# Sixteen layer norms, six gated feed-forwards and two half additions, rewritten block by block, in a single-core transformer kernel

## The chip, the cores and the metric

The kernel runs on one core of a Trainium2 chip. The metric is the device time of one execution, in microseconds. PE is the matrix engine (TensorE), DVE the vector engine, ACT the scalar engine, POOL the general engine (GpSimd) and SP the engine whose queue issues most DMAs. PE, DVE, ACT and POOL each run their own instructions in order and wait for each other through semaphores.

## The reference, cut to what matters

Four layers work on a stream `x` of 16 sequences of 256 tokens with 128 channels. Each layer is feed-forward, attention, feed-forward, each on a layer norm of the stream; the feed-forwards are added at one half.

```python
def _layernorm(x, axis=-1, eps=1e-05):
    m = jnp.mean(x, axis=axis, keepdims=True)
    v = jnp.var(x, axis=axis, keepdims=True)
    return (x - m) / jnp.sqrt(v + eps)
...
# layer 1's feed-forward: two layers, each window attention and then
h = shift_token(x)
mu = h.mean(-1, keepdims=True)
var = h.var(-1, keepdims=True)
h = (h - mu) / jnp.sqrt(var + 1e-05) * lg + lb
h = h @ w1 + b1
a, g = jnp.split(h, 2, axis=-1)
h = a * jax.nn.gelu(g, approximate=False)
x = x + h @ w2 + b2
...
# layer 3's feed-forward
gate = jnp.einsum('bsd,hd->bsh', x, wg)
up = jnp.einsum('bsd,hd->bsh', x, wu)
h = jax.nn.silu(gate) * up
return jnp.einsum('bsh,dh->bsd', h, wd)
...
x = x + 0.5 * _L1_ffn_ref(_layernorm(x, axis=-1), ...)
```

`shift_token` takes the upper 64 channels from the token before (zero for a sequence's first).

## The kernel before

The stream lies in SBUF as `X`, 128 channels on the partitions and 4096 tokens along them; its norm goes to `XN`, of the same shape. Work on tokens goes in `NBLK` = 8 blocks of `BLK` = 512, which is also one PSUM bank in f32. The kernel is a row of phases (class `Phase`): each takes its buffers and semaphores, writes out one program for each engine, and ends in a barrier of all engines. So nothing of a phase overlaps the next, and the time of the kernel is the sum of its phases and of the gaps between them. Every order inside a phase is written out by hand; no scheduler moves anything.

`layer_norm` is called 16 times: 12 plain norms (tags `l0a_norm`, `l0att_norm` and so on, for the six feed-forwards and attentions of layers 0 and 1 and the six of layers 2 and 3), and 4 learned norms inside layer 1's feed-forwards (tags `l1a_ln0`, `l1a_ln1`, `l1b_ln0`, `l1b_ln1`; the profile writes `l1a_ln` and `l1b_ln` for them, the number left out). A plain norm does, for each block s: a matmul with `ones_mean` puts the mean over channels on all partitions of `stat` (L252, PE), DVE subtracts it (`dev`, L269), ACT squares (`sq`, L283), a second matmul gives the variance (L255), ACT takes the logarithm (`log`, L288) and its exponential at -0.5 (`inv`, L291), DVE multiplies (`XN`, L277). PE runs all eight means and then all eight variances; DVE all eight `dev` and then the products; ACT all eight squares, then in each half four logarithms and four exponentials. A learned norm first copies its input to `hs` with the upper 64 partitions shifted by a token (L261 and L262, both on DVE), multiplies by `lg` as well (L274), and ACT adds `lb` in eight last instructions (L296).

`gated_ffn` is called 6 times, 4 times as "gelu" (`l1a_ff`, `l1b_ff`; hidden size 341, in three chunks of 128, 128 and 85) and twice as "int8" (`l3a`, `l3b`; hidden size 384). A loop of 4 trips does `U` = 2 blocks each: for each block and chunk two matmuls `G` and `UP` (L1482, L1483), the gate on ACT (L1500 or L1503), a product on DVE (`hid`, L1530 or L1533); for each block three matmuls back (`OUT`, L1472) and the addition to the stream on DVE (L1518 or L1520). The next trip starts after the second of these additions (`trip_done`). After both of layer 1's inner layers, `add_half` is a phase of its own in which DVE adds half of `XN` to `X` in one instruction of 4096 columns (L1545).

## Time and profile before

| | us |
|---|---|
| median of three runs (6445.07 to 6453.1) | 6449.81 |
| the profiled execution, its own time | 6449.29 |
| its span, first to last instruction | 6447.5 |
| PE busy (32011 matmul instructions) | 4952.8 |
| DVE busy | 4378.2 |
| ACT busy | 3259.1 |
| POOL busy | 2307.3 |

A duration is that of one instruction; where like instructions follow each other, the profile merges them to one row with a count, and the row's duration runs from the first's start to the last's end. An f32 matmul of 512 columns is two PE instructions in the records, so eight of them read x16. What stands in brackets is the idle time of the engine before a row and what ended it. The clock is that which was granted to PE, as a share of its full 2.4 GHz.

### The profile page before, as it was taken

Reading aid. Unit: us, or ns where it says so; the run is one execution under the profiler, and the core shown is the slowest. Engines: PE = TensorE matmul, PEld = TensorE weight load, DVE = VectorE, ACT = ScalarE, POOL = GpSimd, SP = SyncE. Lnnn points to the kernel's source line nnn. Section 1 sums busy time; section 2 is a strip of 40 time slices with the busy share of each in tenths; the row PEclk is TensorE's granted clock in tenths of the full one; section 3 lists DMA queues with packets and bytes.
Section 4 is the critical chain, followed back from the end, with each engine's and each line's share of the span. In section 5 each row is a group of like instructions: output and inputs, shape, how many; then the busy total and the mean of one; then the engine's idle time right before and its main releaser. Section 6 shows DMA issues by size and latency. Waiting matters only on the chain. (4 is left out here: it accounts for less than half of the span.)

```text
span 6447.5 us, 112356 instructions
## 1 busy us (share of the span) xinstructions
PE 4952.8 (77%) x32011; PEld 3318.9 (51%) x32108; DVE 4378.2 (68%) x10756; ACT 3259.1 (51%) x6903; POOL 2307.3 (36%) x1555
## 2 busy tenths in 40 slices
PE   6777888777769879869969879866678657596777
...
GB/s 29 0 0 3 298 287 283 191 0 0 0 11 0 3 11 0 0 9 1 1 11 0 4 11 0 4 8 7 37 17 1 3 12 13 40 0 14 0 0 17
DMA packets 162590, 213.89 MB, mean 33 GB/s; under 512 B 54804, under 2 KB 90984, under 8 KB 162408
## 3 DMA queue, kind: packets, MB, share of 16 engines
...
## 5 line engine op out<-in xcount | busy, mean ns | idle before, releaser
L1841 POOL TENSOR_TENSOR l0b_S<-l0b_sim 128x1024 f32<-128x1024 f32 x256 | 494.1, 1967 | 135.4 <-ACT l0b_sim L1904 113.7
L1841 POOL TENSOR_TENSOR l0a_S<-l0a_sim 128x1024 f32<-128x1024 f32 x256 | 494.2, 1967 | 83.4 <-ACT l0a_sim L1904 62.6
L1876 PE MATMUL l0b_WT<-ident,l0b_w 128*128 128x128 f32 x2048 | 268.9, 287 | 64.0 <-DVE l0b_w L1974 59.4
L1876 PE MATMUL l0a_WT<-ident,l0a_w 128*128 128x128 f32 x2048 | 269.1, 287 | 63.5 <-DVE l0a_w L1974 58.6
L1974 DVE SCALAR_TENSOR_TENSOR l0b_w<-l0b_S,l0b_best,l0b_SG 128x1024 f32<-128x1024 f32 x256 | 311.2, 1276 | 8.3 <-ACT l0b_SG L1921 4.4
L1974 DVE SCALAR_TENSOR_TENSOR l0a_w<-l0a_S,l0a_best,l0a_SG 128x1024 f32<-128x1024 f32 x256 | 311.2, 1276 | 8.2 <-ACT l0a_SG L1921 4.5
L1876 PEld LDWEIGHTS l0b_WT<-ident,l0b_w 128*128 128x128 f32 x2048 | 240.4, 148 | 107.3 <-DVE l0b_w L1974 107.3
L1876 PEld LDWEIGHTS l0a_WT<-ident,l0a_w 128*128 128x128 f32 x2048 | 240.4, 148 | 106.9 <-DVE l0a_w L1974 106.9
L1921 ACT ACTIVATE l0b_SG<-l0b_S 128x1024 f32<-128x1024 f32 x256 | 260.5, 1026 | 55.1 <-DVE l0b_w L1974 50.3
L1921 ACT ACTIVATE l0a_SG<-l0a_S 128x1024 f32<-128x1024 f32 x256 | 260.5, 1026 | 54.1 <-DVE l0a_w L1974 48.9
L2288 ACT ACT_TABLE_LOAD x16 | 20.5, 1283 | 511.6 <-issue 305.5
L772 ACT ACTIVATE l0att_XS<-l0att_XP 128x768 f32<-128x768 f32 x256 | 224.9, 879 | 71.3 <-PE l0att_XP L613 67.7
L793 ACT ACTIVATE l0att_E<-l0att_S,l0att_least 128x256 f32<-128x256 f32 x512 | 232.2, 503 | 29.8 <-DVE l0att_least L861 29.5
L869 DVE COPY l0att_ET<-l0att_TU 128x512 f32<-128x512 f32 x256 | 176.2, 688 | 89.9 <-PE l0att_TU L637 88.9
L861 DVE CUSTOM_DVE_ANT_0 l0att_S<-l0att_SC,l0att_BD 128x256 f32<-128x256 f32 x512 | 196.7, 419 | 29.7 <-issue 24.7
L1251 ACT ACTIVATE l1a_att_E<-l1a_att_S,l1a_att_nmax 128x192 f32<-128x192 f32 (+1 forms) x512 | 195.5, 418 | 10.3 <-DVE l1a_att_nmax L1350 10.3
L1251 ACT ACTIVATE l1b_att_E<-l1b_att_S,l1b_att_nmax 128x192 f32<-128x192 f32 (+1 forms) x512 | 195.4, 418 | 10.3 <-DVE l1b_att_nmax L1350 10.3
L793 ACT ACTIVATE l1att_E<-l1att_S,l1att_least 128x128 f32<-128x128 f32 (+1 forms) x512 | 192.0, 448 | 13.6 <-DVE l1att_least L861 13.6
L1058 POOL TENSOR_TENSOR l1a_att_E<-l1a_att_E,l1a_att_rec 128x768 f32<-128x768 f32 (+1 forms) x96 | 154.5, 1610 | 111.4 <-DVE l1a_att_rec L1359 111.4
L1058 POOL TENSOR_TENSOR l1b_att_E<-l1b_att_E,l1b_att_rec 128x768 f32<-128x768 f32 (+1 forms) x96 | 154.5, 1610 | 111.2 <-DVE l1b_att_rec L1359 111.2
L2375 PE MATMUL l2bc_OUT<-l2bc_hot,l2bc_part 128*128 128x512 bf16 x752 | 167.7, 383 | 16.3 <-DVE l2bc_hot L2407 13.1
L2375 PE MATMUL l2ac_OUT<-l2ac_hot,l2ac_part 128*128 128x512 bf16 x752 | 166.6, 381 | 16.0 <-DVE l2ac_hot L2407 13.1
...
## 6 DMA issues: line engine op xcount, KB each, us to landing
shifted_rows<-l0att_XS SPq DMA_DIRECT2D x256, 384.0 KB, 3.2
l0att_BD<-shifted_rows SPq DMA_DIRECT2D x256, 256.0 KB, 3.4
...
```

Source lines behind the costliest of these rows:

```text
L772: act.activation(XS[:, j % 2, t, :, :].rearrange("p c h -> p h c"), XP[:, :, 0:WIN], ACT.Copy).then_inc(sm["x_kept"], 1)
L793: act.activation(E[:, j % 2, h, t, 0:keys(t)], S[:, j % 2, h, t, 0:keys(t)], ACT.Exp, bias=least[:, j % 2, h, t:t + 1], scale=-1.0).then_i ...
L861: dve.tensor_tensor_reduce(S[:, j % 2, h, t, 0:keys(t)], SC[:, h, t, 0:keys(t)], add, -scale, 3e38, ALU.add, ALU.min, least[:, j % 2, h, t ...
L869: dve.tensor_copy(ET[:, j // 2 % 2, 2 * (j % 2) + h, :, :], TU[:, h % NT, 0:len(blocks), :]).then_inc(sm["et_copied"], 1)
L1058: pool.tensor_tensor(E, E, share, ALU.mult).then_inc(sm["weighed"], 1)
L1251: last = act.activation(out, S[:, b, g * w:(g + 1) * w], ACT.Exp, bias=nmax[:, at_h:at_h + 1], accum_out=total[:, at_h:at_h + 1])
L1841: pool.tensor_tensor(S[:, h, :].rearrange("p (a c) -> p a c", a=NK), a, c, ALU.add).then_inc(sm["summed"], 1)
L1876: o = pe.matmul(WT[:, n // 4, (n % 4) * P:(n % 4 + 1) * P], w[:, h % W_RING, n * P:(n + 1) * P], ident[:, :], start=h == 0 and n % 4 == 0, ...
L1921: act.activation(SG[:, h % SG_RING, :], S[:, h, :], ACT.Sigmoid).then_inc(sm["sigm"], 1)
L1974: dve.scalar_tensor_tensor(w[:, h % W_RING, :], S[:, h, :], best[:, s, h, 7:8], SG[:, h % SG_RING, :], ALU.is_ge, ALU.mult).then_inc(sm["w ...
L2288: act.activation(xT[:, s, :], IO[:, s, 0:P], ACT.Copy).then_inc(sm["copied"], 1)
L2375: o = pe.matmul(OUT[:, :], part[:, k, n, :], hot[:, n % R, :], start=n == 0 and k == 0, stop=False)
```

## The change

Four things are changed. The same numbers are computed.

1. In `layer_norm` each engine's instructions go block by block. PE runs the variance of block s - 2 behind the mean of block s; ACT the square of block s, the logarithm of s - 2 and the exponential of s - 3; DVE the subtraction of block s and the product of s - 4. ACT loads one table set, which holds the logarithm and the exponential, at the start of every norm.
2. In a learned norm the shifted copy of the upper partitions moves to POOL, the copy of the lower ones stays on DVE, three blocks ahead; `lb` is added by DVE (a tensor_scalar behind each product) and no longer by ACT.
3. `gated_ffn` loses its loop of 4 trips and the wait for `trip_done`; all 24 chunks are written out. The matmuls back of a block and its addition come in the next block, behind that block's second chunk.
4. `add_half` and its phase are gone; in the second inner layer of layer 1, DVE adds half of each finished block to `X` right behind the block's own addition.

```diff
@@ layer_norm @@
 pool.memset(by_sequence(hs[64:P, :])[:, :, 0:1], 0.0).then_inc(zeroed, 1)
+for s in range(NBLK):
+    pool.tensor_copy(by_sequence(hs[64:P, at[s]])[:, :, 1:L],
+                     by_sequence(X[64:P, at[s]])[:, :, 0:L - 1]).then_inc(lower, 1)
...
-for s in range(NBLK):
-    pe.matmul(stat[:, s, :], ones_mean[:, :], src[:, at[s]], start=True, stop=True).then_inc(means, 1)
-for s in range(NBLK):
-    pe.wait_ge(squares, s + 1)
-    pe.matmul(stat[:, s, :], ones_mean[:, :], sq[:, s, :], start=True, stop=True).then_inc(vars_, 1)
+for s in range(NBLK + 2):
+    if s < NBLK:
+        if learned:
+            pe.wait_ge(upper, s + 1)
+            pe.wait_ge(lower, s + 1)
+        pe.matmul(stat[:, s, :], ones_mean[:, :], src[:, at[s]], start=True, stop=True).then_inc(means, 1)
+    if s >= 2:
+        pe.wait_ge(squares, s - 1)
+        pe.matmul(stat[:, s - 2, :], ones_mean[:, :], sq[:, s - 2, :], start=True, stop=True).then_inc(vars_, 1)
...
+for s in range(NBLK + 4):
+    if s < NBLK:
+        if learned:
+            if s + 3 < NBLK:
+                stage(s + 3)
...
+        dve.wait_ge(means, s + 1)
+        dve.tensor_tensor(dev[:, s, :], src[:, at[s]], stat[:, s, :], ALU.subtract).then_inc(devs, 1)
+    if s >= 4:
+        b = s - 4
+        dve.wait_ge(devs, b + 1)
+        dve.wait_ge(invs, b + 1)
+        if learned:
+            dve.scalar_tensor_tensor(hs[:, at[b]], dev[:, b, :], lg[:, 0:1], inv[:, b, :], ALU.mult,
+                                     ALU.mult).then_inc(scaled, 1)
+            dve.wait_ge(scaled, b + 1)
+            dve.tensor_scalar(XN[:, at[b]], hs[:, at[b]], lb[:, 0:1], None, ALU.add)
+        else:
+            dve.tensor_tensor(XN[:, at[b]], dev[:, b, :], inv[:, b, :], ALU.mult)
...
+act.preload_act_table_set("natural_log_exp_and_others")
+for s in range(NBLK + 3):
+    if s < NBLK:
+        act.wait_ge(devs, s + 1)
+        act.activation(sq[:, s, :], dev[:, s, :], ACT.Square).then_inc(squares, 1)
+    if 2 <= s < NBLK + 2:
+        act.wait_ge(vars_, s - 1)
+        act.activation(log[:, s - 2, :], stat[:, s - 2, :], ACT.Ln, bias=eps[:, 0:1]).then_inc(logs, 1)
+    if s >= 3:
+        act.wait_ge(logs, s - 2)
+        act.activation(inv[:, s - 3, :], log[:, s - 3, :], ACT.Exp, scale=-0.5).then_inc(invs, 1)
@@ gated_ffn @@
-with pe.Fori(0, NBLK // U) as g:
-    pe.wait_ge(sm["trip_done"], g + 1)
...
+def down(s):
+    pe.wait_ge(sm["hidden"], NC * s + NC)
+    if s >= U:
+        pe.wait_ge(sm["added"], s - U + 1)
...
+for k in range(NBLK * NC):
...
+    if c == 1 and s >= 1:
+        down(s - 1)
+down(NBLK - 1)
...
+def residual(s):
...
+        dve.scalar_tensor_tensor(R[:, at], OUT[:, s % U, :], b2[:, 0:1], R[:, at], ALU.add, ALU.add).then_inc(sm["added"], 1)
+        if into is not None:
+            dve.wait_ge(sm["added"], s + 1)
+            dve.scalar_tensor_tensor(into[:, at], R[:, at], 0.5, into[:, at], ALU.mult, ALU.add)
...
-def add_half(nc, tag, X, Y):
...
-    dve.scalar_tensor_tensor(X[:, :], Y[:, 0:T], 0.5, X[:, :], ALU.mult, ALU.add)
```

How instructions now stand, at three places. The first is ACT's queue in the norm `l0a_norm`, which is that of all twelve plain norms; before:

```order
L283 ACTIVATE l0a_norm_sq<-l0a_norm_dev 128x512 x8
L288 ACT_TABLE_LOAD
L288 ACTIVATE l0a_norm_log<-l0a_norm_stat,eps 128x512 x4
L291 ACT_TABLE_LOAD
L291 ACTIVATE l0a_norm_inv<-l0a_norm_log 128x512 x4
```

and now, its first nine rows:

```order
L294 ACT_TABLE_LOAD
L298 ACTIVATE l0a_norm_sq<-l0a_norm_dev 128x512 x3
L301 ACTIVATE l0a_norm_log<-l0a_norm_stat,eps 128x512
L298 ACTIVATE l0a_norm_sq<-l0a_norm_dev 128x512
L301 ACTIVATE l0a_norm_log<-l0a_norm_stat,eps 128x512
L304 ACTIVATE l0a_norm_inv<-l0a_norm_log 128x512
L298 ACTIVATE l0a_norm_sq<-l0a_norm_dev 128x512
L301 ACTIVATE l0a_norm_log<-l0a_norm_stat,eps 128x512
L304 ACTIVATE l0a_norm_inv<-l0a_norm_log 128x512
```

Of four table loads one is left, at the start, and the three functions take turns. The second is DVE's queue in the learned norm `l1a_ln0`; before, the last rows of the copies and all that follows:

```order
L261 COPY l1a_ln_hs<-XN 64x512
L262 COPY l1a_ln_hs<-XN 64x2x255
L261 COPY l1a_ln_hs<-XN 64x512
L262 COPY l1a_ln_hs<-XN 64x2x255
L269 TENSOR_TENSOR l1a_ln_dev<-l1a_ln_hs,l1a_ln_stat 128x512 x8
L274 SCALAR_TENSOR_TENSOR l1a_ln_sq<-l1a_ln_dev,l1a_ln_lg,l1a_ln_inv 128x512 x8
```

and now, from the middle:

```order
L264 COPY l1a_ln_hs<-XN 64x512
L279 TENSOR_TENSOR l1a_ln_dev<-l1a_ln_hs,l1a_ln_stat 128x512
L264 COPY l1a_ln_hs<-XN 64x512
L279 TENSOR_TENSOR l1a_ln_dev<-l1a_ln_hs,l1a_ln_stat 128x512
L285 SCALAR_TENSOR_TENSOR l1a_ln_hs<-l1a_ln_dev,l1a_ln_lg,l1a_ln_inv 128x512
L288 TENSOR_SCALAR l1a_HX<-l1a_ln_hs,l1a_ln_lb 128x512
L279 TENSOR_TENSOR l1a_ln_dev<-l1a_ln_hs,l1a_ln_stat 128x512
L285 SCALAR_TENSOR_TENSOR l1a_ln_hs<-l1a_ln_dev,l1a_ln_lg,l1a_ln_inv 128x512
L288 TENSOR_SCALAR l1a_HX<-l1a_ln_hs,l1a_ln_lb 128x512
```

The shifted copies have left the queue, and a second instruction follows each product. The third is PE's queue in a gated feed-forward, from the middle of the second block of `l1a_ff`, now:

```order
L1494 MATMUL l1a_ff_G<-l1a_HX,l1a_ff_wg 128x512
L1495 MATMUL l1a_ff_UP<-l1a_HX,l1a_ff_wu 128x512
L1484 MATMUL l1a_ff_OUT<-l1a_ff_hid,l1a_ff_wd 128x512 x3
L1494 MATMUL l1a_ff_G<-l1a_HX,l1a_ff_wg 85x512
L1495 MATMUL l1a_ff_UP<-l1a_HX,l1a_ff_wu 85x512
L1494 MATMUL l1a_ff_G<-l1a_HX,l1a_ff_wg 128x512
L1495 MATMUL l1a_ff_UP<-l1a_HX,l1a_ff_wu 128x512
L1494 MATMUL l1a_ff_G<-l1a_HX,l1a_ff_wg 128x512
L1495 MATMUL l1a_ff_UP<-l1a_HX,l1a_ff_wu 128x512
L1484 MATMUL l1a_ff_OUT<-l1a_ff_hid,l1a_ff_wd 128x512 x3
```

No `OUT` is followed by a wait for its own addition any more; the next chunk's matmuls come right behind it.

## Rows read from the trace of the kernel before

**Rows 1.** View of the core: span and mean granted clock of PE.

```profile
core 0: 6447.5 us, clock 0.874
```

**Rows 2.** Timeline of ACT in `l0a_norm`: start, us, engine, line, op, out<-in, count.

```profile
17.87 0.63 ACT L283 ACTIVATE l0a_norm_sq<-l0a_norm_dev 128x512 f32<-128x512 f32 x1 [2.57 <-DVE l0a_norm_dev L269]
...
23.88 0.63 ACT L283 ACTIVATE l0a_norm_sq<-l0a_norm_dev 128x512 f32<-128x512 f32 x1 [0.23 <-DVE l0a_norm_dev L269]
24.53 1.28 ACT L288 ACT_TABLE_LOAD   x1
25.82 2.43 ACT L288 ACTIVATE l0a_norm_log<-l0a_norm_stat,eps 128x512 f32<-128x512 f32 x4
...
36.80 2.19 ACT L291 ACTIVATE l0a_norm_inv<-l0a_norm_log 128x512 f32<-128x512 f32 x4
```

**Rows 3.** Timeline of DVE in the same norm, the first and the last of it.

```profile
17.15 0.69 DVE L269 TENSOR_TENSOR l0a_norm_dev<-X,l0a_norm_stat 128x512 f32<-128x512 f32 x1 [2.19 <-PE l0a_norm_stat L252]
...
37.47 2.50 DVE L277 TENSOR_TENSOR XN<-l0a_norm_dev,l0a_norm_inv 128x512 f32<-128x512 f32 x4 [4.67 <-ACT l0a_norm_inv L291]
```

**Rows 4.** Timeline of PE in the same norm, all of it.

```profile
16.01 7.10 PE L252 MATMUL l0a_norm_stat<-X,ones_mean 128*128 128x512 f32 x16 [1.35 <-PEq L64]
22.95 7.03 PE L255 MATMUL l0a_norm_stat<-l0a_norm_sq,ones_mean 128*128 128x512 f32 x16
```

**Rows 5.** Timeline of DVE in the learned norm `l1a_ln0`.

```profile
2224.40 0.42 DVE L261 COPY l1a_ln_hs<-XN 64x512 f32<-64x512 f32 x1 [0.96 <-PEq L64]
...
2231.49 4.87 DVE L269 TENSOR_TENSOR l1a_ln_dev<-l1a_ln_hs,l1a_ln_stat 128x512 f32<-128x512 f32 x8
...
2244.28 2.74 DVE L274 SCALAR_TENSOR_TENSOR l1a_ln_sq<-l1a_ln_dev,l1a_ln_lg,l1a_ln_inv 128x512 f32<-128x512 f32 x4 [1.57 <-ACT l1a_ln_inv L291]
```

**Rows 6.** Timeline of ACT in the same learned norm.

```profile
2232.21 4.81 ACT L283 ACTIVATE l1a_ln_sq<-l1a_ln_dev 128x512 f32<-128x512 f32 x8 [13.84 <-DVE l1a_ln_dev L269]
2236.93 2.41 ACT L288 ACTIVATE l1a_ln_log<-l1a_ln_stat,eps 128x512 f32<-128x512 f32 x4
...
2245.66 5.03 ACT L296 ACTIVATE l1a_HX<-l1a_ln_sq,l1a_ln_lb 128x512 f32<-128x512 f32 x8
```

**Rows 7.** Timeline of PE in `l1a_ff`: the phase's start, the turn of a trip.

```profile
2257.17 2.07 PE L1482 MATMUL l1a_ff_G<-l1a_HX,l1a_ff_wg 128*128 x2 [16.11 <-DMA l1a_ff_b<-L_ffn_b]
...
2274.13 2.84 PE L1472 MATMUL l1a_ff_OUT<-l1a_ff_hid,l1a_ff_wd 128*128 128x512 f32 x6 [0.91 <-DVE l1a_ff_hid L1530]
2278.03 1.12 PE L1482 MATMUL l1a_ff_G<-l1a_HX,l1a_ff_wg 128*128 x2 [1.06 <-DVE XN L1518]
...
2295.98 1.12 PE L1482 MATMUL l1a_ff_G<-l1a_HX,l1a_ff_wg 128*128 x2 [1.05 <-DVE XN L1518]
```

**Rows 8.** Timeline of PE in `l3a`: the turn of its first trip.

```profile
5844.73 1.12 PE L1482 MATMUL l3a_G<-XN,l3a_wg 128*128 x2 [1.00 <-DVE X L1520]
```

**Rows 9.** Line L252: ns min/median/max of one, first and last start.

```profile
L252 PE MATMUL l1att_norm_stat<-X,ones_mean x16: 592/592/1192, 2826.0 to 2834.3; 128*128 128x512 f32 x16
L252 PE MATMUL l3att_norm_stat<-X,ones_mean x16: 592/592/667, 5898.8 to 5905.3; 128*128 128x512 f32 x16
```

**Rows 10.** The first 2 us of `l1att_norm`: busy time of each engine, PEclk, DMA share, GB/s.

```profile
2826.00:2828.00 2.00, 1.96 (x3) 0.96 (x4) 0.00 (x0) 0.00 (x0) 0.00 (x0) 0.50 0.06 12
```

**Rows 11.** Groups of like instructions: count | busy us, mean ns of one | idle before.

```profile
L1036 POOL COPY l1a_att_xs<-XN 64x255 f32 x28 | 11.2, 400 | 1.6
L563 POOL CAST l1att_part<-l1att_whole 128x512 bf16<-128x512 f32 x16 | 9.8, 609 | 3.8 <-POOL l1att_whole L571 3.8
...
L2356 POOL TENSOR_TENSOR l2ac_rest<-l2a_Eout,l2ac_part 128x512 f32<-128x512 f32 x8 | 9.7, 1216 | 0.0
L398 DVE TENSOR_SCALAR l2att_E<-l2att_E,l2att_share 128x256 f32<-128x256 f32 x32 | 11.3, 353 | 1.1
```

**Rows 12.** Timeline of all engines around `add_half` of `l1a`.

```profile
2820.64 4.42 DVE L1545 SCALAR_TENSOR_TENSOR X<-XN,X 128x4096 f32<-128x4096 f32 x1 [0.77 <-PEq L64]
2826.04 8.90 PE L252 MATMUL l1att_norm_stat<-X,ones_mean 128*128 128x512 f32 x16 [7.06 <-PEq L64]
```

More of the change, by code:

```diff
@@ L279, in _ @@
             @block.scalar
             def _(act):
-                for s in range(NBLK):
-                    act.wait_ge(devs, s + 1)
-                    act.activation(sq[:, s, :], dev[:, s, :], ACT.Square).then_inc(squares, 1)
-                for half in range(2):
-                    part = range(half * NBLK // 2, (half + 1) * NBLK // 2)
-                    for s in part:
-                        act.wait_ge(vars_, s + 1)
-                        act.activation(log[:, s, :], stat[:, s, :], ACT.Ln, bias=eps[:, 0:1]).then_inc(logs, 1)
-                    for s in part:
-                        act.wait_ge(logs, s + 1)
-                        act.activation(inv[:, s, :], log[:, s, :], ACT.Exp, scale=-0.5).then_inc(invs, 1)
@@ L1417, in _, with gated_ffn @@
                 residual(LAST)
-def gated_ffn(nc, tag, kind, R, XN, W):
+def gated_ffn(nc, tag, kind, R, XN, W, into=None):
     gelu = kind == "gelu"
@@ L1436, in gated_ffn @@
         OUT = ph.ps("OUT", [P, U, BLK])
-        names = "loaded weights_ready gate_made up_made gated hidden out_made trip_done".split()
+        names = "loaded weights_ready gate_made up_made gated hidden out_made added".split()
         sm = {n: ph.sem(n) for n in names}
@@ L1539, in add_half @@
-def add_half(nc, tag, X, Y):
-    with Phase(nc, tag) as ph:
-        with nc.Block() as block:
-            @block.vector
-            def _(dve):
-                dve.scalar_tensor_tensor(X[:, :], Y[:, 0:T], 0.5, X[:, :], ALU.mult, ALU.add)
+                def residual(s):
+                    dve.wait_ge(sm["out_made"], s + 1)
+                    at = slice(s * BLK, (s + 1) * BLK)
+                    if gelu:
+                        dve.scalar_tensor_tensor(R[:, at], OUT[:, s % U, :], b2[:, 0:1], R[:, at], ALU.add, ALU.add).then_inc(sm["added"], 1)
+                        if into is not None:
+                            dve.wait_ge(sm["added"], s + 1)
+                            dve.scalar_tensor_tensor(into[:, at], R[:, at], 0.5, into[:, at], ALU.mult, ALU.add)
+                    else:
+                        dve.scalar_tensor_tensor(R[:, at], OUT[:, s % U, :], 0.5, R[:, at], ALU.mult, ALU.add).then_inc(sm["added"], 1)
@@ new lines, in _ @@
+                for k in range(NBLK * NC):
+                    s, c = k // NC, k % NC
+                    n = width[c]
+                    dve.wait_ge(sm["gated"], k + 1)
+                    dve.wait_ge(sm["up_made"], k + 1)
+                    if s >= U and c == 0:
+                        dve.wait_ge(sm["out_made"], s - U + 1)
+                    if gelu:
+                        dve.scalar_tensor_tensor(hid[0:n, s % U, c, :], UP[0:n, k % 2, :], ba[0:n, c:c + 1],
+                                                 gate_on[0:n, k % 2, :], ALU.add, ALU.mult).then_inc(sm["hidden"], 1)
+                    else:
+                        dve.tensor_tensor(hid[0:n, s % U, c, :], UP[0:n, k % 2, :], gate_on[0:n, k % 2, :],
+                                          ALU.mult).then_inc(sm["hidden"], 1)
+                    if c == 1 and s >= 1:
+                        residual(s - 1)
```

111 lines of the change are left out of this document (31 added, 80 removed).

## The prediction

> **What bounds the kernel now.** The view of the core gives a span of 6447.5 us [rows 1]. The page comes next, but its chain of waits names only the last phase, and its busy shares are means over phases of different kinds. What bounds this kernel is its build: phases behind barriers, so a microsecond taken out of a phase's own chain leaves the total, whatever PE's or DVE's share is. I therefore read the timeline of each kind of phase that the change touches, engine by engine, and asked in each what ends last.
>
> In a plain norm [rows 2 to 4] PE is busy for 13.8 us without a gap, ACT trails, and the end is ACT's: it squares at PE's pace until 24.51, then does four table loads, eight logarithms and eight exponentials, 14.5 us in which PE has work for only the first 5. From PE's first matmul (16.01) to DVE's last product (37.47 + 2.50) the norm takes 23.96 us. In a learned norm [rows 5, 6] there is no table load in the middle, but DVE's sixteen copies come first (7.1 us up to 2231.49) and ACT's eight additions of `lb` last (5.03 us); it takes 26.29 us (2224.40 to 2250.69). A feed-forward [rows 7, 8] runs at PE's pace inside a trip, and PE stands still at the turn.
>
> **Plain norms, 12 of them.** The new pace of a block is the largest of three sums. PE: two matmuls of 512 columns, each two instructions 0.429 apart ((7.03 - 0.592) / 15, [rows 4, 9]), 1.716 us. ACT: a square 0.597 ((4.81 - 0.63) / 7, [rows 6]), a logarithm 0.58 ((2.43 - 0.69) / 3 with 0.69 for one) and an exponential 0.525 (the same from 2.19, [rows 2]), 1.70 us. DVE: a subtraction and a product, 0.69 each at most [rows 3], 1.38 us. So PE sets the pace, with ACT level with it. Counting from PE's first matmul: mean 7 is the thirteenth matmul, at 12 x 0.858 = 10.3; DVE starts on it 1.14 later (16.01 to 17.15), ACT's square 0.72 after that (17.15 to 17.87), at 12.16. Behind it in ACT's order stand a logarithm, an exponential, and so on up to the last exponential: 0.60 + 3 x 0.58 + 3 x 0.525 = 3.92, so it starts at 16.1, the product 0.67 later (36.80 to 37.47) and ends at 17.45. Saved: 23.96 - 17.45 = 6.5, times 12 = **78.0 us**.
>
> New waits in it: DVE now waits for an exponential with the next block's subtraction queued behind, and ACT and PE wait for that one. Square 3 starts at 5.3, so exponential 0, two places behind it, at 6.5, and product 0 ends at about 7.9; subtraction 5 is due at mean 5's 6.86 + 1.14 = 8.0, so it is in time, by 0.1 us; were it late by 0.3 each time, a norm would lose some 1 us. ACT's own table load costs nothing if it is over before the first square at 1.86 after PE's start: it is 1.28 long and ACT has nothing before it. The trace lets ACT go on 0.01 after a load (24.53 + 1.28 to 25.82, [rows 2]). The Trainium skill ("ScalarE: Activation LUTs", What ACT_TABLE_LOAD costs) gives 2.66 us for a switch, 1.28 of load and 1.38 of drain; a norm would then start 0.8 late, 13 us in all for sixteen, and the total would be 6310.
>
> **Warm starts.** The norm behind `add_half` takes 8.3 us from its first mean to its last, the one behind `l3a` 6.5 [rows 9], as its first matmuls take up to 1192 ns, against 667: in its first 2 us the granted clock is 0.50, which is 1.2 GHz [rows 10]. PE has stood still for 7.06 us there, 1.59 in the other. Without `add_half` two norms (`l1att_norm`, `l2a_norm`) follow some 2.5 us behind PE's work: 2 x 1.8 = **3.6 us**, bounds 0 and 3.6. Where PE waits for weights its idle stretch shrinks from 16.11 us [rows 7] to about 11; I give nothing for that.
>
> **Learned norms, 4.** DVE's block is a copy (0.43, for the first eight steps only), a subtraction 0.6, a product 0.70, and the new addition of `lb`, which the trace does not show in this shape: below it the 256-column one at 0.35 [rows 11], above it a 0.75 product; the nearest is the 0.42 of a copy that also reads and writes SBUF [rows 5], so 0.43, and 0.1 for the wait between the two. The shifted copy on POOL lies between 0.61 (a 512-column cast) and 1.22 (two inputs), with twice 0.40 for two runs of 255 between [rows 11]; any of these is under PE's 1.716, so only the first can be on the path, and the first mean comes 1.0 after DVE's first copy as before. Then as in a plain norm, with a start at the slow clock (1.8): the last exponential at 1.0 + 1.8 + 16.1 = 18.9, the one of block 4 2.75 before it. From there DVE is what is late: with block 3's pair in front it takes up block 4 at 17.0 and needs 1.23 for each of four blocks, to 21.9. Saved 26.29 - 21.9 = 4.4, times 4 = **17.6 us**; with `lb` at 0.75 it is 12, with a warm start 24.
>
> POOL and DVE now work side by side on SBUF; nothing in the trace shows that they hinder each other in these shapes. The Trainium skill ("SBUF — State Buffer", SBUF: two separate sides) says they share a port pair as an exclusive lock, which a GpSimd operation and a DVE copy in a two-port mode, or a DVE one with two SBUF inputs, take for the whole instruction. That is the first rival below.
>
> **Feed-forwards, 6.** A trip holds eighteen matmuls of 0.858, 15.45 us, and takes 17.95 (2278.03 to 2295.98, [rows 7]). The missing 2.5 are PE's wait for the last `hid` before `OUT`, and at the turn its wait for the addition. The two waits and the last matmul's run behind its issue make up all of the 2.5, so inside a trip PE never waits for a `hid`, and the new order asks no more of it. Now the next block's matmuls fill both waits, at each of three turns; those of the last block stay. An addition fits behind `OUT`: the next `hid` needs two more matmuls, 1.7 us, first. The new wait of `OUT` for `added` is for a block two before, long done. Gelu: 4 x 3 x 2.5 = **30.0 us**. Int8: the wait at the turn is 1.00 against 1.06 [rows 8], and I take as much off the other, so 2 x 3 x 2.4 = **14.4 us**. The reloaded gate table lay beside PE's first matmul of a trip and is worth nothing. The loads of weights stay.
>
> **The half addition.** Phase and barrier go: from 2819.87 (2820.64 less its 0.77 of idle) the norm begins at 2826.04, 6.17 later [rows 12]; a barrier alone takes 0.98 (2825.06 to 2826.04). 5.2 are saved. Of the eight new additions seven lie in DVE's idle time behind `OUT` (0.75 and a 0.1 wait; the next `hid` is due just as it ends), the last is on the path, 0.8. Twice 4.4 = **8.8 us**.
>
> **Sum.** 78.0 + 3.6 + 17.6 + 30.0 + 14.4 + 8.8 = 152.4. The profiled execution took 6449.3, its span 6447.5, and the median of the runs is 6449.8, so one stands for the other: 6449.3 - 152.4 = **6297 us**.
>
> **The rivals.**
>
> *POOL and DVE take turns in the learned norms.* DVE's eight copies and eight POOL copies in a row, 0.42 + 0.8 each, would hold up the first subtractions by up to three copies (2.4 us) and nothing later. Four times 2.4: 6307. For it speaks that DVE's copies at 0.42 for 512 columns run faster than its 0.69 operations [rows 3, 5], a mode of their own. Chance 0.13.
>
> *ACT does not overlap its three functions.* The 0.58 and 0.525 are from rows of one function in a row. If each took its full 0.63, 0.69 and 0.62 and 0.05 more for its wait, a block would be 2.09 instead of 1.716: 8 x 0.37 = 3 us a norm, 48 in all: 6345. Against it: in the learned norm the squares pass into the logarithms without a gap (2232.21 + 4.81 to 2236.93, [rows 6]). Chance 0.11.
>
> *More comes back than counted.* Shorter idle stretches could spare PE's slow start in the phases behind the norms, too. One start costs 1.8 [rows 9]; in ten of them 18: 6279. Against it: nearly all of these phases begin with their own weight loads. Chance 0.10.
>
> *Slower: the norms' PE falls to half its clock.* PE is now just as fast as ACT. If the short waits between its matmuls brought the granted clock from 2.4 to 1.2 GHz, as after `add_half` [rows 10], a matmul would be 1.716 us, sixteen of them 27.5, and with the 4.6 behind the last a plain norm 32.1, 8.1 more than now. Twelve are 97 us, the learned ones about 27 more, against 53 gained elsewhere: 6520. It decides from a matmul of 1.21 us, where (23.96 - 4.6) / 16 is passed. Against it: PE does not wait 0.1 us between two matmuls by the sum above. Chance 0.02.
>
> *It does not do what it says.* The order shows one table load a norm and the loop gone, so only a cost that no row shows could eat 152 us. Chance 0.02.
>
> **How the numbers follow.** The forecast has 0.62. Its own bounds: `lb` and POOL -6 and +6 us, warm starts -4, a late subtraction -12 (1 us in each norm): 6290 to 6320. With the rivals on both sides, less 2 in 10: 6277 to 6332. About 0.2% (13 us) is what a measurement of this kernel can tell from no change. Every case but the last two is faster by far more: faster 0.96, same 0.01, slower 0.03.
>
> **What would show it.** In `l0a_norm`: from PE's first matmul to the last product 17 to 18 us, PE without gaps, matmuls at 592 ns. If ACT is what is back to back and PE shows gaps, ACT's rival is right. In `l1a_ln0`: about 22 us, DVE without idle time at the end; a first mean later than 1.5 us, or POOL's copies far over 0.8, would be the lock. In `l1a_ff`: the time from PE's first to DVE's last 7.5 us shorter, PE without a wait but before the last `OUT`. `l1att_norm` behind the last addition by under 1 us, its first matmuls at 667. The forecast fails if a block of the norms takes over 2 us.

## The result and the profile after

The changed kernel takes 6302.19 us (median of four runs, 6295.77 to 6302.82), against 6449.72 us for the kernel before (four runs, 6445.07 to 6453.1, on the same chip). The ratio is 0.9772, with a 95% interval of 0.9756 to 0.9787: 147.5 us, or 2.3%, faster. The forecast was 6297, with a range of 6277 to 6332.

The view of the core, kernel after, beside [rows 1]:

```profile
core 0: 6293.7 us, clock 0.882
```

The span is 153.8 us shorter than that of [rows 1]. The norm `l0a_norm` stands for the plain norms. Timeline of ACT in it (start, us, engine, line, op, out<-in, count, idle before), where [rows 2] was before:

```profile
16.12 1.28 ACT L294 ACT_TABLE_LOAD   x1 [0.68 <-PEq L64]
18.01 0.63 ACT L298 ACTIVATE l0a_norm_sq<-l0a_norm_dev 128x512 f32<-128x512 f32 x1 [0.61 <-DVE l0a_norm_dev L279]
...
24.88 0.63 ACT L298 ACTIVATE l0a_norm_sq<-l0a_norm_dev 128x512 f32<-128x512 f32 x1
25.41 0.67 ACT L301 ACTIVATE l0a_norm_log<-l0a_norm_stat,eps 128x512 f32<-128x512 f32 x1
25.98 0.62 ACT L304 ACTIVATE l0a_norm_inv<-l0a_norm_log 128x512 f32<-128x512 f32 x1
26.59 0.63 ACT L298 ACTIVATE l0a_norm_sq<-l0a_norm_dev 128x512 f32<-128x512 f32 x1
```

Timeline of DVE in the same norm (beside [rows 3]):

```profile
25.87 0.69 DVE L279 TENSOR_TENSOR l0a_norm_dev<-X,l0a_norm_stat 128x512 f32<-128x512 f32 x1 [0.19 <-PE l0a_norm_stat L256]
...
32.33 1.29 DVE L290 TENSOR_TENSOR XN<-l0a_norm_dev,l0a_norm_inv 128x512 f32<-128x512 f32 x2 [0.40 <-ACT l0a_norm_inv L304]
```

Timeline of PE in the same norm (beside [rows 4]), its first row, two from the middle, and the last:

```profile
16.16 2.81 PE L256 MATMUL l0a_norm_stat<-X,ones_mean 128*128 128x512 f32 x6 [1.35 <-PEq L64]
...
24.81 1.02 PE L256 MATMUL l0a_norm_stat<-X,ones_mean 128*128 128x512 f32 x2
25.67 1.02 PE L259 MATMUL l0a_norm_stat<-l0a_norm_sq,ones_mean 128*128 128x512 f32 x2
...
27.39 2.74 PE L259 MATMUL l0a_norm_stat<-l0a_norm_sq,ones_mean 128*128 128x512 f32 x6
```

Three things are to be seen. A square, a logarithm and an exponential of ACT start 0.53, 0.57 and 0.61 apart, 1.71 us for a block (24.88 to 26.59), so functions of different kinds overlap like those of one kind. PE's matmuls of 512 columns start 0.86 apart without an idle time, also 1.72 for a block. And from PE's first matmul to the end of DVE's last product it is 32.33 + 1.29 - 16.16 = 17.46 us.

The learned norm `l1a_ln0`: timeline of DVE, its first part and its end (beside [rows 5]):

```profile
2200.25 1.92 DVE L264 COPY l1a_ln_hs<-XN 64x512 f32<-64x512 f32 x3 [0.95 <-PEq L64]
2202.74 0.74 DVE L264 COPY l1a_ln_hs<-XN 64x512 f32<-64x512 f32 x1 [0.56 <-DMA l1a_ln_lb<-L_ffn_ln_b]
2203.41 0.67 DVE L279 TENSOR_TENSOR l1a_ln_dev<-l1a_ln_hs,l1a_ln_stat 128x512 f32<-128x512 f32 x1
2204.00 0.79 DVE L264 COPY l1a_ln_hs<-XN 64x512 f32<-64x512 f32 x1
...
2206.62 0.41 DVE L264 COPY l1a_ln_hs<-XN 64x512 f32<-64x512 f32 x1
...
2217.68 0.75 DVE L285 SCALAR_TENSOR_TENSOR l1a_ln_hs<-l1a_ln_dev,l1a_ln_lg,l1a_ln_inv 128x512 f32<-128x512 f32 x1 [0.68 <-ACT l1a_ln_inv L304]
2218.46 0.49 DVE L288 TENSOR_SCALAR l1a_HX<-l1a_ln_hs,l1a_ln_lb 128x512 f32<-128x512 f32 x1
2218.86 0.75 DVE L285 SCALAR_TENSOR_TENSOR l1a_ln_hs<-l1a_ln_dev,l1a_ln_lg,l1a_ln_inv 128x512 f32<-128x512 f32 x1
...
2222.01 0.49 DVE L288 TENSOR_SCALAR l1a_HX<-l1a_ln_hs,l1a_ln_lb 128x512 f32<-128x512 f32 x1
```

Timeline of POOL in the same norm, its only row but the memset:

```profile
2200.39 5.43 POOL L244 COPY l1a_ln_hs<-XN 64x510 f32<-64x510 f32 x8
```

Line L264 in this norm, all of DVE's copies but the last (count: ns min/median/max of one, first and last start):

```profile
L264 DVE COPY l1a_ln_hs<-XN x7: 410/745/828, 2200.3 to 2206.6; 64x512 f32<-64x512 f32 x7
```

The norm takes 2222.50 - 2200.25 = 22.25 us, against 26.29 before. DVE's first copy starts before POOL's first and takes 0.42 us; the next five, beside POOL's copies (until 2205.82), take 0.62 to 0.83, and the two after them 0.41.

The feed-forward `l1a_ff`: timeline of PE, its start, the place where a trip used to turn, and the end (beside [rows 7]):

```profile
2229.17 2.08 PE L1494 MATMUL l1a_ff_G<-l1a_HX,l1a_ff_wg 128*128 128x512 f32 x2 [11.51 <-DMA l1a_ff_b<-L_ffn_b]
2231.03 1.67 PE L1495 MATMUL l1a_ff_UP<-l1a_HX,l1a_ff_wu 128*128 128x512 f32 x2
...
2247.16 2.74 PE L1484 MATMUL l1a_ff_OUT<-l1a_ff_hid,l1a_ff_wd 128*128 128x512 f32 x6
2249.74 1.02 PE L1494 MATMUL l1a_ff_G<-l1a_HX,l1a_ff_wg 128*85 128x512 f32 x2
...
2291.17 2.85 PE L1484 MATMUL l1a_ff_OUT<-l1a_ff_hid,l1a_ff_wd 128*128 128x512 f32 x6 [0.91 <-DVE l1a_ff_hid L1542]
```

PE waits nowhere after its first matmul but before the last `OUT`. Last, `l1att_norm` behind it. Line L256 in this norm (beside [rows 9]), and busy time by windows of 2 us (us; busy of PE, PEld, DVE, ACT and POOL with counts; PEclk; DMA share; GB/s):

```profile
L256 PE MATMUL l1att_norm_stat<-X,ones_mean x16: 592/592/1061, 2770.3 to 2782.8; 128*128 128x512 f32 x16
```

```profile
2768.00:2770.00 2.00, 0.03 (x1) 0.00 (x0) 1.44 (x2) 0.00 (x0) 0.00 (x0) 1.00 0.00 0
2770.00:2772.00 2.00, 1.72 (x4) 1.01 (x5) 0.58 (x1) 1.28 (x1) 0.00 (x0) 0.91 0.00 0
2772.00:2774.00 2.00, 2.00 (x3) 0.68 (x2) 0.79 (x2) 1.16 (x2) 0.00 (x0) 0.50 0.00 0
2774.00:2776.00 2.00, 2.00 (x5) 0.80 (x4) 0.69 (x1) 0.92 (x3) 0.00 (x0) 0.74 0.00 0
2776.00:2778.00 2.00, 2.00 (x6) 0.87 (x5) 0.69 (x1) 1.12 (x3) 0.00 (x0) 1.00 0.00 0
```

Here PE had stood still for 2.26 us, and the norm did not start warm as forecast, nor cold as in [rows 10]: it starts at the full clock, falls to 0.50 (1.2 GHz) while PE is already busy, and comes back.

### The profile page after: what moved, and what is told of

Its sections match the earlier page's. It is cut to its first block and busy times, and to the rows that moved or that the text cites. A ratio compares the mean times of both kernels' runs of the same rounds, so it can differ in the third digit from the quotient of the medians.

```text
span 6293.7 us, 111726 instructions
## 1 busy us (share of the span) xinstructions
PE 4931.9 (78%) x32011; PEld 3306.1 (53%) x32108; DVE 4393.4 (70%) x10770; ACT 3163.2 (50%) x6821; POOL 2330.4 (37%) x1587
## 3 DMA queue, kind: packets, MB, share of 16 engines
q1 hardware_dynamic: 160360, 207.73, 10.4%
## 5 line engine op out<-in xcount | busy, mean ns | idle before, releaser
L2291 ACT ACT_TABLE_LOAD x16 | 20.5, 1283 | 511.7 <-issue 305.4
L1260 ACT ACTIVATE l1b_att_E<-l1b_att_S,l1b_att_nmax 128x192 f32<-128x192 f32 (+1 forms) x512 | 194.8, 418 | 10.2 <-DVE l1b_att_nmax L1359 10.2
L1260 ACT ACTIVATE l1a_att_E<-l1a_att_S,l1a_att_nmax 128x192 f32<-128x192 f32 (+1 forms) x512 | 194.8, 418 | 10.2 <-DVE l1a_att_nmax L1359 10.2
L2378 PE MATMUL l2ac_OUT<-l2ac_hot,l2ac_part 128*128 128x512 bf16 x752 | 168.0, 384 | 16.1 <-DVE l2ac_hot L2410 13.1
```

The source lines that it names most:

```text
L1260: last = act.activation(out, S[:, b, g * w:(g + 1) * w], ACT.Exp, bias=nmax[:, at_h:at_h + 1], accum_out=total[:, at_h:at_h + 1])
L2291: act.activation(xT[:, s, :], IO[:, s, 0:P], ACT.Copy).then_inc(sm["copied"], 1)
L2378: o = pe.matmul(OUT[:, :], part[:, k, n, :], hot[:, n % R, :], start=n == 0 and k == 0, stop=False)
```

## The experiments

### The sum, taken apart

The ratio of each run is against the kernel before on the same chip: median 6440.04 us for the first four runs, 6449.84 for the next three, 6445.53 for the last three. The figures expected in us were reckoned from 6449.8 or from 6302, so with the first four it is the differences that are to be compared. Three kernels each carry one part of the change into the kernel before.

**One table load in place of four.** The norms of before, with one line more:

```diff
@@ layer_norm of the kernel before, ACT @@
+act.preload_act_table_set("natural_log_exp_and_others")
 for s in range(NBLK):
```

> The kernel before, with one table set loaded at the start of every norm and nothing else changed. If the four table loads are what the plain norms wait for, ACT's last exponential starts at 24.53 + 8 x 0.58 + 7 x 0.525 = 32.8 in l0a_norm and the norm takes 18.2 us in place of 23.96: 12 x 5.7 = 69 us, 6381. If the order by blocks is what brings the gain (the rival), the loads were in part beside other waits and the run stays above 6425. The learned norms had no load in them and stay at 26.3 us either way.

Measured: 6389.71 us (6384.4 to 6399.12), ratio 0.9922 (0.9900 to 0.9944). Timeline of ACT in its `l0a_norm`:

```profile
16.43 1.28 ACT L281 ACT_TABLE_LOAD   x1 [0.68 <-PEq L64]
...
24.33 0.63 ACT L284 ACTIVATE l0a_norm_sq<-l0a_norm_dev 128x512 f32<-128x512 f32 x1 [0.23 <-DVE l0a_norm_dev L269]
24.87 2.00 ACT L289 ACTIVATE l0a_norm_log<-l0a_norm_stat,eps 128x512 f32<-128x512 f32 x3
```

The logarithms follow the squares at once, and the norm takes 18.70 us (`l0a_norm`, PE's first matmul to the last product) against 23.96. So 5.3 of the 6.5 us that a plain norm gains come from the tables, and another 1.2 from the order by blocks on top of them. What that order would bring with the tables still switched, no run shows. The twelve plain norms sum to 237.9 us here, against 296.9 and 302.7 in the two traces of the kernel before: 59 to 65 less, where 69 were expected. The median is 50.3 lower than that of the kernel before, with 14 to either side by the interval: the 69 expected lie outside it, what the norms save in the traces at its upper end. The learned norms stayed at 26.27 us. Four loads less on the path for 5.26 us are 1.3 each: the 1.28 of the load and hardly more. The Trainium skill ("ScalarE: Activation LUTs", What ACT_TABLE_LOAD costs) gives 2.66 for a switch with its drain; four of them would be 10.6 a norm, an estimate from that page. No drain shows here.

**The new norms alone**: the whole `layer_norm` of the change, with the loop of the feed-forwards and `add_half` as before.

```diff
@@ the kernel before @@
-for s in range(NBLK):
-    pe.matmul(stat[:, s, :], ones_mean[:, :], src[:, at[s]], start=True, stop=True).then_inc(means, 1)
...
+for s in range(NBLK + 2):
...
+for s in range(NBLK + 4):
...
+for s in range(NBLK + 3):
...
```

> The kernel before, with the new norms alone; the feed-forward loop and the phase of the half addition stay. The plain norms give 74 us (17.5 to 20 us each), the learned ones 4 x 4 = 16: 6360. If the 1.3 us by which PE's slow start of each feed-forward got shorter comes from the shorter idle time in front of it, it shows here too, with the old loop (first chunk to first OUT 10.3 us in place of 11.6) and the run is at 6352; if it comes from the new order of the feed-forward, that stretch stays at 11.6.

Measured: 6358.65 us (6351.01 to 6368.83), ratio 0.9874 (0.9852 to 0.9896), 81 us below the kernel before, where 90 and 98 were expected. The profile speaks for neither figure: its feed-forwards reach their first `OUT` 10.4 to 11.7 us after the first `G`, those of the kernel before 10.2 to 11.7 in its two traces, so this stretch does not go with the idle time in front of it. Its plain norms sum to 221.1 us, about as in the kernel after, and its learned norms take 22.25.

**The new feed-forwards alone**: the whole `gated_ffn` of the change, with the norms of before; `add_half` stays.

```diff
@@ the kernel before @@
-with pe.Fori(0, NBLK // U) as g:
-    pe.wait_ge(sm["trip_done"], g + 1)
...
+for k in range(NBLK * NC):
...
+down(NBLK - 1)
```

> The kernel before, with the feed-forwards written out and nothing else changed. Three turns of 2.5 us (2.4 in int8) go from each: 44 us, 6405. If the new order also shortens PE's slow start (first chunk to first OUT 10.3 us in place of 11.6), it is 52 us, 6398.

Measured: 6397.49 us (6384.76 to 6410.14), ratio 0.9936 (0.9913 to 0.9958). It is 42.6 us below the kernel before, where 44 and 52 were expected; the interval does not choose between them. The lengths say more: its six feed-forwards take 65.6 to 66.3 us from PE's first `G` to DVE's last addition, 394.7 in all against 445.1 and 440.6 in the two traces of the kernel before. They reach their first `OUT` after 10.3 to 10.9 us, which the kernel before, with the old loop, also does in five of six in its second trace. So the new order saves the turns, and no shorter start is shown to come from it.

**The half addition back as a phase**, in the kernel after:

```diff
@@ the kernel after @@
-gated_ffn(nc, f"{tag}_ff{n}", "gelu", XN, HX, w, X if n == 1 else None)
+gated_ffn(nc, f"{tag}_ff{n}", "gelu", XN, HX, w)
...
+add_half(nc, tag + "_add", X, XN)
```

> The changed kernel, with the half addition as a phase of its own again. Theory: a phase of 4.42 us and a barrier come back, 0.8 us of last addition goes, twice: 9 us more than the changed kernel, 6311. Rival: PE's start of the norms behind it was slow in both, so nothing is added there; if it were slower by 1.8 us each with 7 us of idle time, 6314.

Measured: 6312.04 us (6294.66 to 6320.94), ratio 0.9801 (0.9778 to 0.9824). This interval overlaps that of the kernel after (0.9756 to 0.9787), so the medians do not show the 9 us. Against the kernel before on the same chip it is 128 us faster, near the 81 + 43 of the two parts above. The 9 us are read from the lengths: from the last addition of the feed-forward to the norm's first matmul it is 5.8 us here, twice; in the kernel after 1.5. `l1att_norm` and `l2a_norm` begin at 1.2 GHz, as behind the phase in the kernel before; line L256 in the first of them:

```profile
L256 PE MATMUL l1att_norm_stat<-X,ones_mean x16: 592/592/1192, 2766.6 to 2779.3; 128*128 128x512 f32 x16
```

### POOL and DVE

**The shifted copies back on DVE**, POOL silent, all else as in the kernel after:

```diff
@@ layer_norm of the kernel after @@
-for s in range(NBLK):
-    pool.tensor_copy(by_sequence(hs[64:P, at[s]])[:, :, 1:L], ...).then_inc(lower, 1)
...
 def stage(s):
     dve.tensor_copy(hs[0:64, at[s]], X[0:64, at[s]]).then_inc(upper, 1)
+    dve.tensor_copy(by_sequence(hs[64:P, at[s]])[:, :, 1:L], ...).then_inc(lower, 1)
```

> The changed kernel, with the shifted copies of the learned norms on DVE again, each behind its block's other copy, and POOL silent. If DVE's copies took 0.74 us because POOL's copies ran beside them, every copy is at 0.42 here; DVE then has 16 x 0.43 = 6.9 us of copies against 8 copies in about 5.1 us, so a learned norm is 0 to 1.5 us longer than its 22.3: 6302 to 6308. If they are slow for another reason (the rival), they stay near 0.74 and a norm takes over 25 us: above 6312.

Measured: 6299.87 us (6290.75 to 6302.53), ratio 0.9769 (0.9753 to 0.9786), not to be told from the kernel after. Timeline of DVE in its `l1a_ln0`, three rows from its first part:

```profile
2192.24 0.69 DVE L278 TENSOR_TENSOR l1a_ln_dev<-l1a_ln_hs,l1a_ln_stat 128x512 f32<-128x512 f32 x1
2192.85 0.41 DVE L261 COPY l1a_ln_hs<-XN 64x512 f32<-64x512 f32 x1
2193.29 0.42 DVE L262 COPY l1a_ln_hs<-XN 64x510 f32<-64x510 f32 x1
```

All copies take 0.41 or 0.42 when POOL is silent, so it is POOL that stretches them to between 0.62 and 0.83 in the kernel after. They are held up until a copy of POOL is over: in the nine traces in which POOL copies, each of the 173 DVE copies over 0.5 us ends 0.28 us after the end of one of POOL's. The subtraction, which reads one input from SBUF and one from PSUM, is 0.67 there and 0.69 here: it is not held up. That is what the Trainium skill says ("SBUF — State Buffer", SBUF: two separate sides): a copy in a two-port mode and a GpSimd operation exclude each other. But it costs less than the copies that POOL takes off: the learned norm takes 22.98 us in this kernel and 22.25 in the kernel after. Over four norms that is 2.9 us, too little for these medians.

### The clock at the start of a phase

**Two more matmuls behind the last `OUT`**, unused, so that PE stands still for a shorter time before the next norm:

```diff
@@ gated_ffn of the kernel after, PE @@
 down(NBLK - 1)
+pe.wait_ge(sm["gated"], NBLK * NC)
+for k in range(2):
+    pe.matmul(G[:, k, :], wg[:, 0:P], XN[:, 0:BLK], start=True, stop=True)
```

> The changed kernel, with two more matmuls of 1.7 us in all behind the last OUT of each feed-forward, whose result nobody reads; they lie beside DVE's last additions. If the idle time in front of a norm (2.26 us before l1att_norm and l2a_norm) sets PE's clock at its start, it is now under 1.3 us, these two start at 667 ns and are 1.7 us shorter: 3.4 us, 6299. If the clock at the start goes by something else (l2att_norm and l3a_norm, both behind 1.64 us of idle, started at 1061 and 667), nothing changes in a fixed way: 6302.

Measured: 6302.58 us (6297.6 to 6311.53), ratio 0.9776 (0.9759 to 0.9792): as a time, no gain. In the trace, what was expected of the idle time is seen. Line L256 and the timeline of PE at the start of `l1att_norm`:

```profile
L256 PE MATMUL l1att_norm_stat<-X,ones_mean x16: 592/592/667, 2766.5 to 2777.4; 128*128 128x512 f32 x16
```

```profile
2766.55 2.81 PE L256 MATMUL l1att_norm_stat<-X,ones_mean 128*128 128x512 f32 x6 [0.74 <-PEq L64]
```

Both norms take 17.5 us, at the full clock throughout. The matmuls make the barrier 0.2 us later, and 1.7 us gained at each of two places are too little for these medians. One trace is thin evidence, too: both norms start at full clock here and in the last kernel below, four of four, but without the matmuls seven of twelve do (the table below), and at that share four in a row would come by chance once in nine.

**Weights loaded ahead.** The nine loads of a gelu feed-forward (three of an int8 one) move into the norm in front of it:

```diff
@@ kernel after @@
-layer_norm(nc, f"{tag}_ln{n}", XN, HX, ones_mean, eps, (w["ln_g"], w["ln_b"]))
-gated_ffn(nc, f"{tag}_ff{n}", "gelu", XN, HX, w, X if n == 1 else None)
+bufs, ahead = ffn_weights(held, nc, f"{tag}_ff{n}", "gelu", w)
+layer_norm(nc, f"{tag}_ln{n}", XN, HX, ones_mean, eps, (w["ln_g"], w["ln_b"]), ahead)
+gated_ffn(nc, f"{tag}_ff{n}", "gelu", XN, HX, w, X if n == 1 else None, bufs)
@@ layer_norm, SP @@
+for dst, w in ahead:
+    load(sp, dst, w, fetched)
+if ahead:
+    sp.wait_ge(fetched, 16 * len(ahead))
```

> The changed kernel, with the weights of each feed-forward loaded during the norm in front of it (its SP queue is idle there, and a norm of 17 to 22 us is longer than the 6 us of the loads). The feed-forward then starts right behind its barrier: 5.5 us less in each gelu one, 4 in each int8 one, 30 us in all: 6272. If PE's shorter idle time (5 to 6 us in place of 11.5) also lets it start at full clock, 1.7 us more in each: 6262. Rival: the loads in the norm delay its own small loads of lg and lb, or a barrier waits for them, and the gain is under 15 us: above 6287.

Measured: 6268.34 us (6260.54 to 6276.18), ratio 0.9715 (0.9699 to 0.9731); once more, together with the next two kernels, 6269.06 (6266.83 to 6275.74), ratio 0.9724 (0.9710 to 0.9737). This is faster than both kernels, by what was expected of the earlier start alone (6272). Timeline of PE at the start of `l1a_ff`:

```profile
2225.32 2.04 PE L1501 MATMUL l1a_ff_G<-l1a_HX,l1a_ff_wg 128*128 128x512 f32 x2 [5.62 <-PEq L64]
2227.16 1.91 PE L1502 MATMUL l1a_ff_UP<-l1a_HX,l1a_ff_wu 128*128 128x512 f32 x2
2228.86 1.73 PE L1501 MATMUL l1a_ff_G<-l1a_HX,l1a_ff_wg 128*128 128x512 f32 x2
```

PE stands still for 5.62 us instead of 11.51, but the start is not warmer: three pairs of matmuls are slow here, where above only two were. From the first `G` to the first `OUT` the gelu feed-forwards of this kernel take 11.1 to 11.5 us in its two traces, those of the kernel after 10.3 to 10.7 in the first and up to 11.7 in the second. For the clock, the shorter idle time of 5.2 to 6.0 us brings nothing.

**The same, with PE kept busy to the end of the norm.** What was expected of the run of comparison:

> The kernel after with the feed-forwards' weights loaded during the norm in front, once more, for a direct comparison: 6268 by its first run. If the extra matmuls are worth 14 us, it is 14 above them here. The starts of the feed-forwards again 10.3 to 11.5 us to the first OUT.

```diff
@@ layer_norm, PE, with the weights loaded ahead @@
         pe.matmul(stat[:, s - 2, :], ones_mean[:, :], sq[:, s - 2, :], start=True, stop=True).then_inc(vars_, 1)
+pe.wait_ge(logs, 1)
+for _ in range(5 if learned else 4):
+    pe.matmul(stat[:, 0, :], ones_mean[:, :], sq[:, 0, :], start=True, stop=True)
```

> The kernel after with the feed-forwards' weights loaded during the norm in front of them (as in the run where they came ahead), and in each of the sixteen norms four more matmuls on PE behind the last variance (five in the learned ones), into a statistics bank that nobody reads any more. They compute nothing that is used. Theory: what PE does in the last microseconds sets the clock with which the next phase starts. With 5.6 us of idle time a gated feed-forward takes 11.1 to 11.4 us to its first OUT, of which the ten matmuls at full clock are 8.6; with the extra matmuls PE stands still for under 1.5 us, and those phases start at full clock: 4 x 2.7 + 2 x 1.8 = 14 us less than 6268, so 6254, and if attention phases gain as well down to 6240. Rival: the idle time at the barrier is enough to lose the clock whatever comes before, or the matmuls delay the norm's last logarithms: 6268 or more.

Measured: 6263.22 us (6249.62 to 6268.97), ratio 0.9713 (0.9697 to 0.9728). Timeline of PE around the start of `l1a_ff`, and its first 2 us by windows:

```profile
2219.82 4.46 PE L269 MATMUL l1a_ln_stat<-l1a_ln_sq,ones_mean 128*128 128x512 f32 x10
2225.60 1.10 PE L1504 MATMUL l1a_ff_G<-l1a_HX,l1a_ff_wg 128*128 128x512 f32 x2 [1.32 <-PEq L64]
2226.53 1.02 PE L1505 MATMUL l1a_ff_UP<-l1a_HX,l1a_ff_wu 128*128 128x512 f32 x2
```

```profile
2225.60:2227.60 2.00, 2.00 (x5) 1.03 (x6) 0.00 (x0) 1.93 (x2) 0.00 (x0) 1.00 0.00 0
```

All six feed-forwards now reach their first `OUT` in 8.66 to 8.69 us, that is ten matmuls at 0.86, and take 64.0 us in all, against 65.5 to 66.9 in the two traces without the extra matmuls: 14 to 15 us over the six, the 14 that were expected. The norms do not get longer by it (22.24 us the learned ones). The medians differ by 5.8 us only, and their intervals overlap; the spans of the two profiled executions differ by 17 (6256.6 against 6273.6), but the one without the matmuls is the slowest of its five. That the starts are at full clock is shown (idle for 1.3 to 1.7 us in front of them, where it was 5.2 to 6.0); how much of the 15 us arrives in the time is not settled by five runs each.

The last kernel adds the two matmuls behind each `OUT` as well:

> The same, and two more unused matmuls behind each feed-forward's last OUT. Theory: the two norms behind them (l1att_norm, l2a_norm) always start at full clock, where without them it was slow in some executions and full in others (17.5 against 19.2 us): 0 to 3.4 us less, the later barrier 6 x 0.2 = 1.2 more: 6253 against 6254. Rival: the two matmuls cost more than they bring, 6256 or more. The difference of the two is inside what the medians can tell; the lengths of the norms in the trace decide.

Measured: 6266.31 us (6256.52 to 6274.24), ratio 0.9715 (0.9700 to 0.9731): not to be told from the one before. `l1att_norm` and `l2a_norm` both take 17.5 us, but in the same execution `l3b_norm` took 20.5 instead of 17.5. The second execution of the kernel before, without any edit, shows the same at the same place: 26.9 instead of 23.9. That is the subject of the last two runs.

### What changes between two executions

> The kernel before, once more, for its profile alone: how much do phases that nobody changed differ between two profiled executions? Between the profiles of before and after, the rel attention of layer 0 took 7.1 us more and the experts of layer 0 together 7.9 less, with the same instructions. If these are effects of the change, this run repeats the times of before (attention 620.3 us from norm end to norm start, within 1 us). If they are chance of an execution, it lies elsewhere.

> The kernel after once more, unchanged, one look: total 6302 within 8. It shows which stretches change from one execution to the next: the starts of phases where PE had stood still for 1.4 to 2.3 us are expected to differ (first matmuls at 1.2 or 2.4 GHz), those behind 1.35 us or less, or behind more than 6 us, to be the same.

Measured: 6439.45 us for the kernel before, 6305.25 for the kernel after, and spans of 6437.6 and 6303.1, so 9.9 below and 9.4 above the first ones. From `l0att_norm`'s last product to `l0b_norm`'s first matmul, which no edit touches, it was 620.3 and 623.6 us in the two traces of the kernel before and 627.4 and 624.7 in those of the kernel after: not the same within 1 us, so part of the 7.1 that seemed an effect of the change is chance. Timeline of PE in `l1a_ff` of the kernel before, second execution, beside [rows 7]:

```profile
2253.39 2.07 PE L1482 MATMUL l1a_ff_G<-l1a_HX,l1a_ff_wg 128*128 x2 [16.15 <-DMA l1a_ff_b<-L_ffn_b]
2255.25 1.77 PE L1483 MATMUL l1a_ff_UP<-l1a_HX,l1a_ff_wu 128*128 x2
2256.86 1.02 PE L1482 MATMUL l1a_ff_G<-l1a_HX,l1a_ff_wg 128*128 x2
```

The idle time is the same as in [rows 7], but here the third row is fast: 10.34 us to the first `OUT`, against 11.59 in the first execution. The twelve norms' starts, over all fourteen traces of this study (the longest of a norm's first matmuls in ns, 667 being the full clock):

| PE's idle time before the norm | where | at full clock |
|---|---|---|
| 0.74 to 0.96 us | `l1att`, `l2a`, `l3att` with the extra matmuls | 6 of 6 |
| 1.33 to 1.36 | `l0a`, `l0att`, `l1a` | 42 of 42 |
| 1.48 to 1.60 | `l3att` | 12 of 12 |
| 1.63 to 1.65 | `l3a` | 10 of 14 |
| 1.63 to 1.92 | `l2att` | 4 of 14 |
| 2.06 to 2.07 | `l3b` | 12 of 14 |
| 2.25 to 2.49 | `l1att`, `l2a` without the phase | 7 of 12 |
| 6.6 to 7.06 | `l1att`, `l2a` behind `add_half` | 0 of 12 |
| 1.44 to 1.45 | `l2b` | 3 of 14 |
| 1.43 to 1.80 | `l1b` | 0 of 14 |
| 1.51 to 1.53 | `l0b` | 0 of 14 |

So the idle time alone does not decide. `l0b` is always slow after 1.5 us, and there the granted clock had fallen before the norm came, with PE only partly busy (1.31 of 2 us) at the end of the phase in front: over the last 2 us before the norm it was 0.50 in thirteen traces and 0.67 in the other. The same holds at `l1b` (0.50 to 0.76 in all fourteen) and at `l2b` (0.50 to 0.57 in the eleven traces with a start at 1.2 GHz, 1.00 in the other three). Where `l1att`, `l2a`, `l2att` and `l3a` are slow without `add_half` in front, it is otherwise: the clock was 1.00 up to the start and fell after it.

Nor is it all chance of an execution. Three kernels have two traces each: the kernel before, the kernel after, and the one with the weights ahead. Of these 36 pairs of starts four differ: `l2b` in each of the first two kernels, `l3b` in the kernel before and `l2a` in the kernel after. As expected, no start behind 1.36 us or less or behind more than 6 changed, but most of those behind 1.4 to 2.3 us did not change either. At `l2att` and `l3a` all three pairs are alike, and `l3a` is slow in exactly the four traces with the old feed-forward loop: there the start goes with the kernel. Why, no run shows. Busy time by windows of the kernel after, shortly before `l0att_norm` (PE's first matmul at 585.6, full clock) and shortly before `l0b_norm` (1230.5, slow):

```profile
582.20:584.20 2.00, 1.95 (x16) 1.86 (x16) 1.63 (x9) 0.00 (x0) 0.00 (x0) 1.00 0.00 0
...
1226.50:1228.50 2.00, 1.31 (x5) 0.91 (x6) 0.55 (x2) 0.00 (x0) 0.00 (x0) 0.50 0.00 0
```

Phases that no edit touches change as well: from `l0att_norm`'s last product to `l0b_norm`'s first matmul it was 614.7 to 629.3 us in the fourteen traces, from `l2att_norm` to `l2b_norm` 155.6 to 164.3. Why, no run here shows.

## Why the prediction was right, point by point

The terms, measured on both executions of each kernel, so that the chance of a start weighs less (sums of lengths in us, first and second execution):

| term | before | after | saved | forecast |
|---|---|---|---|---|
| plain norms with their starts | 296.9, 302.7 | 222.6, 217.4 | 79.8 | 81.6 |
| learned norms | 4 x 26.29, 4 x 26.27 | 4 x 22.25, 4 x 22.25 | 16.1 | 17.6 |
| feed-forwards | 445.1, 440.6 | 394.1, 396.0 | 47.8 | 44.4 |
| last addition to the norm, twice | 12.0, 12.0 | 2.9, 2.9 | 9.1 | 8.8 |
| sum | | | 152.8 | 152.4 |

The medians differ by 147.5, the mean spans by 144.2 (6442.6 and 6298.4); the 8.6 us between that and 152.8 lie in phases that the change does not touch. They are of the size by which one such phase alone varies, and I can't tell chance from a small loss there. That the sum of the terms meets the forecast within 0.4 us is luck: the norms gave 3.3 less than forecast and the feed-forwards 3.4 more, and most of those 3.4 come from starts that were slower in the kernel before, for which the forecast had nothing.

- **The pace of a norm** was right: 1.72 us a block, PE and ACT level, 17.46 us against 17.45 computed. The sum did not say where the 6.5 come from; the first experiment does: 5.3 from table loads, and 1.2 more with the pipeline on top. The waits were as read, too: in the steady part DVE's subtraction waits 0.19 for its mean and never comes late. ACT's load (16.12 to 17.40) is over 0.61 before the first square.
- **Warm starts** failed. The step "two norms follow some 2.5 us behind PE's work: 2 x 1.8" took the 667 ns of `l3att_norm` behind 1.59 us for the rule at 2.26. There the clock was at full in 7 of 12 starts, and at `l2a_norm` it differs between two executions of the same kernel. In the profiled pair `l1att_norm` and `l2a_norm` were slow with the change (19.2 us each) as without it: a slow start cost 1.7 in place of 1.8 to 2.0, so the term was near its lower bound, 0. The row of [rows 9] from one execution could not carry it.
- **Learned norms**: 22.25 against 21.9, so 4.0 a norm and not 4.4. The addition of `lb` took 0.49, forecast 0.43, and POOL's copy 0.68, forecast 0.8. The last four pairs came at 17.43 after the start instead of 17.0, and took 4.82 instead of 4.9. Two things in front were not counted: a wait of 0.56 for the load of `lb`, and the stretched copies. POOL's copies take 0.61 to 0.81 one by one; 0.68 is their distance in a row.
- **POOL and DVE take turns** is true as a mechanism and wrong as a price. It was to cost 2.4 us a norm; the norm is 0.35 over the forecast with all causes together. A likely reason, not tested, is that the copies are issued three blocks ahead and that PE, at its slow clock, was not there yet.
- **ACT does not overlap its functions**: refuted by the 1.71 us of a block.
- **Feed-forwards**: over the two executions of the kernel before, a gelu one is 73.2 to 74.6 us, by the time at which the clock came back; with the slow first matmuls equal (73.3 and 65.7 for `l1a_ff`) the change saves 7.6, forecast 7.5. What the first pair shows beyond it (74.54 to 65.64, 8.9) is a start that happened to be 1.3 longer before. The waits went as said: none but that before the last `OUT`.
- **More comes back**: this rival did not come true. That a shorter idle stretch before the feed-forwards would spare the slow start was not seen in any trace. At 11.5 us and at 5.6 the first matmuls are at 1.2 GHz all the same; at 1.3 to 1.7, with matmuls up to the end of the norm, they are at 2.4.
- **The half addition**: gap of 1.46 in place of 6.16 and 5.86, so 4.7 and 4.4, forecast 4.4.
- **Slower, at half the clock**: did not occur; PE shows no wait between two matmuls of a plain norm, and one of 0.43 in `l1a_ln0`, before its last variance.
